# Two attentions written out without loops, row maxima planned three steps ahead, the causal row mask moved to VectorE

## The reference

```
# first: 32 heads of 16, each with its own k and v
scores = einsum('bhqd,bhkd->bhqk', q, k) / sqrt(16);  attn = softmax(scores);  out = attn @ v
# second: 32 query heads, one shared k and v head of 16
scores = einsum('bqhd,bkd->bhqk', q, k) * 16**-0.5 + slopes * (pos_k - pos_q)
probs  = softmax(where(pos_k <= pos_q, scores, -1e30));  attn = probs @ v
```

## Time and profile before

| | |
|---|---|
| runs | 2365.27, 2366.73, 2372.2 us; median 2366.73 |
| profiled execution | 2357.78 us, its span 2356.0 us, mean granted TensorE clock 0.921 |
| busy over the span | PE 2091.7 us (89%), DVE 1475.3 (63%), ACT 1146.4 (49%), POOL 134.0 (6%) |
| B: first row units, steps | 42.3 us, 711.7 us |
| G: first row units, steps | 31.3 us, 576.2 us |

### The profile page before, as it was taken

One profiled execution on the slowest core, in us unless ns is written; L12 is line 12 of the kernel. 1 busy time (PEld: TensorE's weight loads), 2 busy tenths in 40 slices (PEclk: granted clock), 3 DMA queues, 4 the chain that ended last, 5 costly groups with the idle time before them and its releaser, 6 DMA issues. The chain is left out here.

```text
span 2356.0 us, 39663 instructions
## 1 busy us (share of the span) xinstructions
PE 2091.7 (89%) x13072; PEld 1233.5 (52%) x13072; DVE 1475.3 (63%) x2004; ACT 1146.4 (49%) x2399; POOL 134.0 (6%) x171
## 2 busy tenths in 40 slices
PE   7987999999999998869999995789898989998785
PEld 5763333333333332748888874545455555545564
DVE  5317988887888882754333315367676666753677
ACT  3211777776777777223222211226665656663153
POOL 0000000000000000210000000000000000000203
PEclk9995999999999999979999997969998889986888
DMA  5443422422332310342100003421111111101411
GB/s 205 161 148 42 61 36 34 58 38 33 51 46 33 47 23 13 113 152 68 37 1 36 4 16 129 146 53 35 37 47 32 39 44 27 47 3 54 144 66 72
DMA packets 100890, 143.37 MB, mean 61 GB/s; under 512 B 32084, under 2 KB 43220, under 8 KB 100720
## 3 DMA queue, kind: packets, MB, share of 16 engines
q1 hardware_dynamic: 99520, 138.91, 23.2%
q10 hardware_dynamic: 832, 1.41, 0.4%
q0 software_dynamic: 384, 0.77, 0.1%
HBM read 93.45 MB, written 47.05 MB: 60 GB/s over the span
## 5 line engine op out<-in xcount | busy, mean ns | idle before, releaser
L730 DVE TENSOR_REDUCE maxesB<-s_psB 128x1 f32<-128x1024 f32 x512 | 603.1, 1220 | 116.3 <-PE s_psB L779 115.4
L714 ACT ACTIVATE probsB<-st_psB 128x512 f32<-128x512 f32 x1024 | 528.9, 603 | 171.5 <-PE st_psB L793 171.3
L730 DVE TENSOR_REDUCE maxesG<-s_psG 128x1 f32<-128x896 f32 (+7 forms) x512 | 368.9, 754 | 185.0 <-PE s_psG L764 180.5
L714 ACT ACTIVATE probsG<-st_psG 128x512 f32<-128x512 f32 (+3 forms) x768 | 335.0, 492 | 244.0 <-PE st_psG L764 180.4
L793 PE MATMUL st_psB<-q_stackB,k_stackB 50*128 50x512 f32 x1024 | 401.0, 474 | 17.2 <-ACT probsB L714 6.8
L779 PE MATMUL s_psB<-k_stackB,q_stackB 48*128 48x512 f32 x1024 | 336.7, 449 | 31.7 <-DMA k_stackB<-k_parts 18.7
L779 PE MATMUL s_psG<-k_stackG,q_stackG 52*128 52x512 f32 (+3 forms) x768 | 263.9, 426 | 65.3 <-DVE maxesG L730 38.8
L793 PE MATMUL st_psG<-q_stackG,k_stackG 54*128 54x512 f32 (+3 forms) x768 | 315.1, 463 | 6.2 <-ACT probsG L714 4.5
L779 PEld LDWEIGHTS s_psB<-k_stackB,q_stackB 48*128 48x128 f32 x1024 | 162.7, 196 | 283.8 <-DVE maxesB L730 235.9
L815 PE MATMUL o_psB<-probsB,v_onesB 128*32 128x512 f32 x2048 | 279.0, 613 | 0.0
L793 PEld LDWEIGHTS st_psB<-q_stackB,k_stackB 50*128 50x128 f32 x1024 | 169.6, 187 | 135.7 <-ACT probsB L714 132.4
(11 more groups left out here) (241 smaller groups left out, 2925.1 us busy)
## 6 DMA issues: line engine op xcount, KB each, us to landing
q_stackB<-q_parts SPq DMA_DIRECT2D x186, 64.0 KB
k_stackB<-k_parts SPq DMA_DIRECT2D x93, 128.0 KB
q_stackG<-q_parts SPq DMA_DIRECT2D x186, 64.0 KB
q_parts<-partsA SPq DMA_DIRECT2D x16, 512.0 KB, 2.8
k_parts<-partsA SPq DMA_DIRECT2D x16, 512.0 KB, 2.8
q_parts<-partsF SPq DMA_DIRECT2D x16, 512.0 KB, 2.8
k_stackG<-k_parts SPq DMA_DIRECT2D x93, 64.0 KB
xA<-in_x SPq DMA_DIRECT2D x4, 1024.0 KB
```

What stands on the lines that cost most here:

```text
L714: act.activation(probs[:, (i % ring) * GH + h, first:HALF], st_ps[:, bank_of(n), first:HALF], ACT.Exp).then_inc(st_used, 1)
L730: dve.reduce_max(maxes[:, half, h * QT + qt:h * QT + qt + 1], s_ps[:, n % 2, 0:key_width(half, qt)], AX.X).then_inc(maxed, 1)
```

## The change

- **Loops.** In both attentions all groups are written out on every engine; the loop counters, `settle` and two semaphores go.
- **Plan of row units.** `plan_units` deals the units over all steps of all groups by their width, so that each half's maxima are complete about three steps (`LEAD`) before use. In B 44 half-units come before step 0 and four in each step; group it+1 begins at step 5 of group it. In G 30 units come before step 0, and group it+1 begins at step 1 of group it. Turns follow at steps 5 and 13 of a group in B, and at 1 and 5 in G. No units are left from step 244 of 256 in B and 182 of 192 in G.
- **First attention.** A unit is 512 keys wide; DVE takes a maximum of each half of a row tile into `part_maxes`, and one small maximum a turn joins them. `s_ps` is a ring of four banks.
- **Second attention.** The row mask matmuls go (1024 of them). DVE adds a constant `ramp` (zeros, with the mask in its last 128 columns) and takes the maximum in one operation that also writes the sum as bf16 to `junk`. The copies of `o_ps` go from DVE to ACT.
- **Step order.** `step_order` mixes rows, keys and masks by the side of the array they use (partitions 0 to 63, 64 to 127).
- **SP.** In a group it now writes the max rows of the first half, waits for the last key scores of the group before, loads the stacks of **it+1** and the values of it+1, and writes the max rows of the second half. Group 1's stacks are still loaded at the start.
- `v_ones` has two buffers. `ramp` (512 KB) is one more constant loaded on SP in phase A, ahead of the weights.

```diff
-            def body(it, buf, before):
-                if before:
-                    sp.wait_ge(st_made, 1 + n_takes * it)
-                max_rows(2 * it + 1, 1, buf)
-                if not is_last(it, 2):
-                    sp.wait_ge(stacks, n_loads * (it + 2))
-                    settle(sp, sp_passed)
-                    load_stacks(sp, it + 2, (buf + 2) % 3)
...
-                if not is_last(it):
-                    max_rows(2 * it + 2, 0, (buf + 1) % 3)
...
+            for it in range(ITS):
+                max_rows(2 * it)
+                if it:
+                    sp.wait_ge(st_made, max(exps_of[first_of[2 * it] - 1]) + 1)
+                if it and it < ITS - 1:
+                    sp.wait_ge(stacks, n_loads * (it + 1))
+                    load_stacks(sp, it + 1)
+                if it < ITS - 1:
+                    sp.wait_ge(v_set, it + 2)
+                    load_v(it + 1)
+                max_rows(2 * it + 1)
...
             def maximum(n):
                 t, qt, h, x = units[n]
                 width = key_width(t % 2, qt)
...
+                if causal:
+                    if n >= JUNK and n % (JUNK // 2) == 0:
+                        dve.wait_ge(maxed, n - JUNK // 2)
+                    dve.tensor_tensor_reduce(junk[:, n % JUNK, 0:width], scores, ramp[:, SEQ - width:SEQ], 1.0, LOWEST, ALU.add,
+                                             ALU.max, out).then_inc(maxed, 1)
+                else:
+                    dve.reduce_max(out, scores, AX.X).then_inc(maxed, 1)
...
             def row_scores(n, part):
                 t, qt, h, x = units[n]
                 it, half = divmod(t, 2)
                 a, b = (k + x * HALF for k in row_parts(t, qt)[part])
+                if n % (2 * UNITS) == 0 and part == 0:
+                    pe.wait_ge(stacks, n_loads * (it + 1))
+                if part == 0 and slot_before[n] >= 0:
+                    pe.wait_ge(maxed, slot_before[n] + 1)
...
+    def plan_units():
+        work = [key_width(t % 2, qt) + FIXED for t, qt, *_ in units]
+        done = list(itertools.accumulate(work))
+        group = first_of[2]
+        per_step = done[2 * UNITS - 1] / group
+        ahead = max(done[UNITS * (t + 1) - 1] - per_step * max(first_of[t] - LEAD, 0) for t in range(1, 3))
+        ahead = max(ahead, done[UNITS - 1])
+        at = [[] for _ in steps]
+        before = []
+        for n, d in enumerate(done):
+            i = int(-(-(d - ahead) // per_step)) - 1
+            (before if i < 0 else at[min(i, len(steps) - 1)]).append(n)
+        return before, at
```

More of the change, by code:

```diff
@@ L540, in beside @@
[L540 to L556, removed]
@@ L580, in last_exp, with key_width @@
[L580 to L592, removed]
+    def key_width(half, qt):
+        return (half * QT + qt + 1) * P if causal else HALF
+    TURNS = 2 * ITS
+    UNITS = GH * QT * (2 if halved else 1)
@@ new lines, in heads_of @@
+    def heads_of(i):
+        last = ("mask", 1) if steps[i][4] else ("key",)
+        return [item[1] for item in step_order(i) if item[:1] + item[2:] == last]
+    turn_after = {}
+    for t in range(TURNS):
+        i = max([j for j, ns in enumerate(units_at) if any(units[n][0] == t for n in ns)], default=-1)
+        if i >= 0:
+            turn_after[i + 1] = turn_after.get(i + 1, []) + [t]
+    early_turns = [t for t in range(TURNS) if not any(t in ts for ts in turn_after.values())]
+    takes = [("max", t, 0) for t in early_turns]
@@ L593, in attention @@
+    for i in range(len(steps)):
+        takes += [("exp", i, h) for h in heads_of(i)]
+        takes += [("max", t, 0) for t in turn_after.get(i, ())]
+    where = {take: n for n, take in enumerate(takes)}
+    exps_of = [[where["exp", i, h] for h in range(GH)] for i in range(len(steps))]
     n_loads = 16 * SIDES * (3 * len(Q_PARTS) + (2 if causal else 0))
     n_rows = 16 * SHIFT * SIDES
[L595 to L605, removed]
@@ L694, in _ @@
+            for i, (it, half, kt, *_) in enumerate(steps):
+                for t in turn_after.get(i, ()):
+                    split_max(t)
+                if i - first_of[2 * it] == 1 and it < ITS - 1:
+                    spread(it + 1)
         @block.scalar
         def _(act):
[L696 to L709, removed]
-                        continue
-                    first = steps[i][2]
-                    if where[("exp", i, h)] == min(where[("exp", i, o)] for o in range(GH)) and (before or i >= ring):
-                        act.wait_ge(pv_done, n_steps * it + i - ring + 1)
-                    act.activation(probs[:, (i % ring) * GH + h, first:HALF], st_ps[:, bank_of(n), first:HALF],
-                                   ACT.Exp).then_inc(st_used, 1)
@@ new lines, in copy_o @@
+            def copy_o(t):
+                act.wait_ge(pv_done, first_of[t + 1])
+                act.activation(ot(*divmod(t, 2)), o_ps[:, :], ACT.Copy).then_inc(o_out, 1)
+            load_stacks(act, 0, range(1, SIDES))
+            for t in early_turns:
+                take_max(t)
+            for i, (it, half, kt, *_) in enumerate(steps):
+                exps(i)
+                if causal and kt == 0 and i:
+                    copy_o(2 * it + half - 1)
+                for t in turn_after.get(i, ()):
+                    take_max(t)
@@ new lines, in _ @@
+            for n in before:
+                for part in range(len(row_parts(*units[n][:2]))):
+                    row_scores(n, part)
+            for t in early_turns:
+                turn_max(t)
+            for i, (it, half, kt, *_) in enumerate(steps):
+                if kt == 0:
+                    pe.wait_ge(m_rows, n_rows * (2 * it + half + 1))
+                for kind, *which in step_order(i):
+                    if kind == "row":
+                        row_scores(*which)
+                    elif kind == "key":
+                        key_scores(i, *which)
+                    else:
+                        mask_keys(i, *which)
+                if i:
+                    values(i - 1)
+                for t in turn_after.get(i, ()):
+                    turn_max(t)
```

368 lines of the change are left out of this document (180 added, 188 removed).

## The result

| | before | changed |
|---|---|---|
| median of the runs | 2366.0 us (2354.3 to 2372.2, 4 runs) | 2517.0 us (2509.0 to 2542.7, 4 runs) |
| profiled execution, clock | 2357.78 us, 0.921 | 2509.02 us, 0.875 |
| B, first units and steps | 42.3 + 711.7 us | 31.5 + 704.9 us |
| G, first units and steps | 31.3 + 576.2 us | 26.4 + 746.9 us |

A forecast was written before the change was run, and what follows sets the result against it. It took B's pace as the cycle from key scores through exps to values, with PE waiting for late stacks in G. G +166, its first units -2, B -25.6, phase A +1.5: +139.9, so 2506 us; range 2415 to 2600.

The forecast's parts named there:

- The wait in G: Groups 1 to 14 of G: PE waits for late stacks at step 1, 9.0 us each (7.5 to 10), 126 us.
- What a stall costs through the clock: G: each PE stall costs 8 us (2.5 to 13) beyond itself through low clock, priced from loop ends.
- A warm group of 30.5 us: G: a group at full clock without the wait takes 30.5 us (27.5 to 33.3), against 33.31 before.
- more even dealing lets it run: G: DVE needs 28 to 29 us a group, and evenly dealt row units let it run, supporting 30.5 us a group.
- The masked maximum: DVE in G: full rate, plus 0.15 us a unit (0.06 to 0.19) for writing the accumulator, 4.8 us a group.
- Rival C: G: masked maximum runs at half rate on DVE, group 55 us, +292 us, 2632 us in all; chance 0.05.
- rival B: G: clock stays at 1.2 GHz throughout, group 53 us, +243 us, 2583 us in all; chance 0.14.
- B: First attention: loop ends -16.6 and start -9 us, other terms 0; sum -25.6 us, bounds -45 and +40.
- The turn with two steps to go: B: turns have 5.4 us where the chain needs 5.4 to 6.3; 0 to +28 us, taken as 0.
- First units of G: Before G's steps: units drop from 32 to 30, without masks, -2 us.
- phase A: Start of kernel: `ramp`, 0.5 MB, loads ahead of the weights, +1.5 us (0 to 3).
- Rival A: G: the stall costs only itself as PE catches up, group 36 us, 2341 us in all; chance 0.08.

The follow-up runs named there:

- the experiment made for it: Kernel before with all groups written out as straight code, G's stacks of it+1 loaded only in group it, so PE waits at group heads: 2589 us.

## Why the prediction was right

The time and the chain of cause were right: stacks loaded a group late make PE wait 14 times in G, and the clock falls behind these waits. That the total came within 11 us is in part luck, since one term was right as a sum of two wrong parts.

- **The wait in G**, 9.0 us, 14 times, forecast from issue times: 9.6 us, 14 times, at step 1. Right; shown by the two kernels with the stacks two groups ahead, in which it is gone. Its parts were less right: the stacks were there 13.4 us after the first issue, not 12.5, from 9.9 us of issue (11.1 forecast) and 3.5 to landing (1 to 1.5).
- **What a stall costs through the clock**, 8 us from the loop ends: 7.6 us in the experiment made for it. Right as the mean price of a stall by itself, where single stalls cost 3.5 to 4 or 9 to 15 us.
- **A warm group of 30.5 us**: wrong in its place here. Without any late stacks the changed order takes 39.1 us on the mean of 15 groups (587 us), 34.8 at best; the old order, with the mask moved too, takes 31.1 at full clock. And in the changed kernel the two costs don't add: with the waits a group takes 47.7 us (668 us in 14), 9.6 of it wait, so 38.1, no more than without them. The low clock that the stall brings seems to fall on stretches that have it anyway; no run tests that. Forecast were 30.5 + 8 = 38.5 for the same part. So the forecast 665 us met 668 by the term "warm group" being too small by what "clock" was too large. The step that failed is "more even dealing lets it run": the order inside a step was not even, PE waited for exps (38.4 us with it, 3.9 without), and the clock fell; with the old order fifteen groups take 62 us less.
- **The masked maximum**: forecast 0.15 us a unit beyond a plain one, measured 0.083. Rival C is out: the row of two tensors was the right nearest one, and the measured rate agrees. The Trainium skill ("Vector Engine (DVE) Microarchitecture Reference", section "7. Points that are easy to get wrong") names the half rate for two sources in SBUF that are not bf16; here one is in PSUM, and the 689 ns agree with that. What the move of the mask costs through the clock, 35 to 41 us in the old order, the forecast didn't have: it called fewer matmuls a gain, and only rival B named them as a danger. The price is not a firm one: the kernel with old dealing and order but the mask moved, 2310 us, is 15 us above the one with the whole old second attention.
- **B**, forecast -25.6, came to -17.6. The start is 31.5 us (33 forecast). The stacks came 1.1 us late at step 5, 16 us in all, where I had given them 0.4 us to spare. The term that was mis-sized is the time until they are in place: 15 to 16 us after the first issue (258.95 to 274.11 the first time), not 13.5. Against that a group without such a wait is 0.8 us shorter (42.6 us), because the loops went, which I had counted by their ends alone. Three of the 14 waits were followed by 3 to 4 us at clock 0.50; the mean stayed at 0.99.
- **The turn with two steps to go**, given 0 in B: at most 0.2 us in B. In G six groups wait 1.7 us at a half's start.
- **First units of G** -4.9 (forecast -2), phase A +1.1 (+1.5).
- **Rival A** is out: groups with a wait take 43.9 us at best, not 36. **Rival B** nearly holds for one group of the 14 (57.2 us at 0.56). Its factor was miscounted: 17.87 over 12.05 is 1.48, not 1.45, so its group would be 54 us.

What stays open: why the clock falls in one group and not in the next with the same instructions, as in the alternating groups above, or at the end of B in one kernel and not in another; and which part of the time lost by the changed order is the order's own waits and which the clock's.

## What to carry to other kernels

When a consumer is moved earlier in a plan, walk its inputs back: here the row units went half a group ahead, the loads that feed them went a whole group back, and the third buffer stood empty. Price a stall of TensorE with the low-clock stretch that follows it, read from stalls that the profile already has, and don't add that price to a stretch that is at the low clock for another reason. A plan that counts columns can still send two matmuls into banks that the next engine frees one by one; judge an order by what PE waits for and by the clock it keeps, not by its evenness. And when a forecast is met, take its terms apart all the same: here two wrong ones made a right sum.

## What was not expected of the hardware

- Four waits of 0.4 to 0.7 us within 5 us were followed by the same low clock as one wait of 3 to 12 us, once for 3.5 us and once for 24. Of 14 single waits in B, 1.1 us on the mean, three were followed by it, for 3 to 4 us, and the longest, 1.76 us, was not. Four waits of 0.35 to 0.73 us in a group, 3 us or more apart, left the clock at 1.00 in the kernel before written out.
- Taking 64 small matmuls a group off PE made the kernel 35 to 41 us slower, with a low clock in eight of 15 groups, while putting them back in an order that has lulls gained nothing.
- Loops cost more than their ends: straight code took 1.2 us off each group of B and 0.64 off each of G besides.
